# Recommender tower on one Trainium2 core: an early period's layer 0 on VectorE, one unit held back, turnings moved

## The reference, cut to what matters

```python
e = jnp.stack([tbl_0[ids[:, 0]], ..., tbl_31[ids[:, 31]]], axis=1)   # (1024, 32, 16)
x0 = xk = e
for W in (W0, W1, W2):                       # (32, 32, 64), then (32, 64, 64) twice
    xk = relu(einsum('bmd,bhd,mhk->bkd', x0, xk, W))
    outs.append(sum(xk, axis=2))
z = concatenate(outs, axis=1)                # (1024, 192)
h = concatenate([z, dense_ctx], axis=1)      # (1024, 208)
y = relu(relu(h @ W_top1 + b_top1) @ W_top2 + b_top2) @ W_top3
```

## Time and profile before

| | before |
|---|---|
| median of 3 runs | 640.38 us (640.11 to 641.25) |
| profiled execution | 638.23 us |
| its span, first to last instruction | 636.4 us |
| PE busy | 585.1 us, 92% |
| DVE busy | 581.5 us, 91% |
| POOL busy | 443.0 us, 70% |
| ACT busy | 371.1 us, 58% |
| mean granted TensorE clock | 0.984 |

### The profile page before, as it was taken

The page is one execution under the profiler, slowest core; times in us unless marked ns, Lnnn a source line. Parts: engine busy times, 40 slices in busy tenths (PEclk is TensorE's granted clock), DMA queues, the critical chain, the costliest instruction groups (busy, mean ns, idle before and its releaser), DMA issues.

```text
span 636.4 us, 8226 instructions
## 1 busy us (share of the span) xinstructions
PE 585.1 (92%) x3030; PEld 220.0 (35%) x3030; DVE 581.5 (91%) x347; ACT 371.1 (58%) x641; POOL 443.0 (70%) x416
## 2 busy tenths in 40 slices
PE   0678788699898989999999999999999999999998
PEld 0244532233232323333334323333334323334355
DVE  2279976898999999999999999999999999999995
ACT  1147552846756565747676575747676575737551
POOL 6477788797888878886979688886989592703012
PEclk9769999899999999999999999999999999999999
DMA  6663897938293845749291846748391947500000
GB/s 172 183 187 58 318 230 240 340 68 304 60 260 132 214 194 126 283 73 335 49 304 60 212 196 143 266 95 314 61 320 36 233 170 176 234 1 1 0 1 1
DMA packets 33365, 105.85 MB, mean 166 GB/s; under 512 B 8999, under 2 KB 16173, under 8 KB 29485
## 3 DMA queue, kind: packets, MB, share of 16 engines
q1 hardware_dynamic: 24044, 102.72, 51.2%
q0 software_dynamic: 8192, 2.11, 2.7%
q10 hardware_dynamic: 1088, 0.49, 0.4%
HBM read 89.56 MB, written 15.73 MB: 165 GB/s over the span
## 4 chain that ended last, share of the span: by engine, by line
DVE 47%; PE 30%; issue 13%; POOL 7%; DMA 2%; ACT 0%; DVEq 0%; ACTq 0%; POOLq 0%
DVE prod L636 47%; PE accb L757 10%; PE acca L757 9%; POOL emb L470 7%; PE acc L698 3%; DMA emb<-in_table,idx 2%; PE spread L804 2%; PE accb L782 1%; PE acc L782 1%; PE acc L728 1%; PE spread L799 1%; PE spread L800 0%; DMA idx<-in_ids 0%; ACT x1a L959 0%; PE spread L682 0%
## 5 line engine op out<-in xcount | busy, mean ns | idle before, releaser
L470 POOL DMA_INDIRECT emb<-in_table,idx x256 | 244.8, 956 | 81.6 <-issue 68.9
L757 PE MATMUL acca<-prod,w 128*64 128x512 f32 x960 | 215.0, 594 | 4.1 <-DVE prod L636 3.3
L757 PE MATMUL accb<-prod,w 128*64 128x512 f32 x896 | 203.3, 600 | 15.5 <-DVE prod L636 15.5
L636 DVE TENSOR_TENSOR prod<-rows,x1a 128x2048 f32<-128x2048 f32 x64 | 145.5, 2279 | 11.5 <-ACT x1a L959 5.2
L636 DVE TENSOR_TENSOR prod<-rows,x2a 128x2048 f32<-128x2048 f32 x64 | 145.5, 2278 | 5.6 <-ACT x2a L959 4.9
L636 DVE TENSOR_TENSOR prod<-rows,x1b 128x2048 f32<-128x2048 f32 (+1 forms) x65 | 145.5, 2245 | 2.6 <-PE accb L757 1.9
L636 DVE TENSOR_TENSOR prod<-rows,x2b 128x2048 f32<-128x2048 f32 x64 | 145.5, 2278 | 1.1 <-PE accb L757 1.1
L757 PEld LDWEIGHTS acca<-prod,w 128*64 128x64 f32 x960 | 67.2, 137 | 137.0 <-issue 127.0
L757 PEld LDWEIGHTS accb<-prod,w 128*64 128x64 f32 x896 | 61.9, 137 | 149.5 <-issue 107.2
L488 POOL TENSOR_TENSOR prod<-rows,mates 128x1024 f32<-128x1024 f32 x42 | 99.2, 2380 | 4.9 <-DMA rows<-field_dram 4.7
L959 ACT ACTIVATE x1a<-acc 64x512 f32<-64x512 f32 x58 | 33.1, 570 | 95.1 <-PE acc L698 94.4
(11 more groups left out here) (105 smaller groups left out, 349.1 us busy)
## 6 DMA issues: line engine op xcount, KB each, us to landing
rows<-field_dram SPq DMA_DIRECT2D x30, 2048.0 KB, 11.3
field_dram<-zb_field SPq DMA_DIRECT2D x30, 256.0 KB, 3.2
mates<-field_dram SPq DMA_DIRECT2D x15, 512.0 KB, 4.6
across<-field_dram SPq DMA_DIRECT2D x56, 128.0 KB
emb<-in_table,idx POOLq DMA_INDIRECT x256, 4.9
field_dram<-zb_field SPq DMA_DIRECT2D x30, 128.0 KB, 4.1
rows<-field_dram SPq DMA_DIRECT2D x4, 768.0 KB, 7.2
field_dram<-zb_field SPq DMA_DIRECT2D x15, 192.0 KB, 4.4
```

The costliest lines, as they stand in the source:

```text
L470: pool.indirect_dma_start(out=emb[q % EMBS][:, j * EMB:(j + 1) * EMB], out_offset=None, in_=table, in_offset=bass.IndirectOffsetOnAxis(ap= ...
L636: nc.vector.tensor_tensor(prod[:, n % RING, t:t + count, :], of_rows, xs, ALU.mult).then_inc(s_prod, 1)
L757: mm = nc.tensor.matmul(acc[j % 2][side * HID:(side + 1) * HID, :], (w1 if layer == 1 else w2)[:, step, :], prod[:, (made(layer, s, half, ...
```

## The change

- `EARLY_PERIODS` goes from 2 to 3: DVE makes five products for period 2, right after the eight units of slot 2. POOL makes none for it, SP reads neither `across` nor `squares` for it, and ACT squares nothing for it.
- DVE's unit 15, the last of `FIRST_UNITS`, comes after the products of period 1 and not before them, and PE contracts it after the layer 0 of period 1.
- Slot 3's units alternate between the streams, as in the other slots.
- Layer 0 of period 3 is summed one pair earlier on PE: after the first and second pair of slot 4.
- PE turns the fields of period 1 one unit earlier, and those of period 2 inside the layer 0 of period 1, after its second step.
- ACT's `fields_out(1)` comes before `first_input(1, 1, 1)` (the x2b that units 8 and 9 read), and `first_z(2, 1)` after `input1(3, 0)`.
- `keep_busy` on PE: 8 and not 6 after the first turning, one more before the second turning, 3 before unit 0, and 2 after the layer 0 of period 2.

```diff
-    EARLY_PERIODS = 2
+    EARLY_PERIODS = 3
...
-        if j == FIRST_SLOT + 1:
-            return [(*stream, half, u) for half in range(2) for stream in (a, b) for u in range(UNITS)]
...
-    SUM0 = {(FIRST_SLOT, 3): [(k, 2) for k in (*range(L0 - 1), SQUARES, L0 - 1)]}
+    SUM0 = {(FIRST_SLOT, 3): [(k, 2) for k in range(EARLY)]}
...
-        late = q == 3
-        SUM0[2 * q - 2, late] = [(k, q) for k in range(3)]
-        SUM0[2 * q - 2, 1 + late] = [(SQUARES, q), (L0 - 1, q)]
+        SUM0[2 * q - 2, 0] = [(k, q) for k in range(3)]
+        SUM0[2 * q - 2, 1] = [(SQUARES, q), (L0 - 1, q)]
...
-        return q < 2
+        return q < EARLY_PERIODS
...
-            sp.wait_ge(s_prod0p, (PERIODS - 2) * L0)
+            sp.wait_ge(s_prod0p, (PERIODS - EARLY_PERIODS) * L0)
...
             halve12(0)
-            for k in range(L0):
-                product0(2, k)
             gather_early(4)
...
-            for i, unit in enumerate(FIRST_UNITS):
+            for i, unit in enumerate(FIRST_UNITS[:-1]):
                 outer(*unit)
...
             for k in range(EARLY):
                 product0(1, k)
+            outer(*FIRST_UNITS[-1])
             for j in range(FIRST_SLOT, SUBS):
                 for unit in vector_units(j):
                     outer(*unit)
+                if j == FIRST_SLOT:
+                    for k in range(EARLY):
+                        product0(2, k)
...
-            keep_busy(acc[1][:, :], 6)
+            keep_busy(acc[1][:, :], 8)
             pe.wait_ge(s_w0sum, 3)
             for k in range(EARLY):
                 layer0_first(k, 0)
                 if k == 1:
+                    keep_busy(acc[1][:, :], 1)
                     turn_first(1)
-            for i, unit in enumerate(FIRST_UNITS):
+            keep_busy(acc[1][:, :], 3)
+            for i, unit in enumerate(FIRST_UNITS[:-1]):
                 outer_alone(*unit)
...
-                if i == 3 * UNITS - 1:
+                if i == 3 * UNITS - 2:
                     turn_fields(1, 0)
-                if i == len(FIRST_UNITS) - 2:
-                    turn_fields(2, 0)
             for k in order0(1):
                 layer0(k, 1)
+                if k == 1:
+                    turn_fields(2, 0)
+            outer_alone(*FIRST_UNITS[-1])
...
                     for k, q in SUM0.get((j, i), []):
                         layer0(k, q)
+                    if (j, i) == (FIRST_SLOT, 2 * UNITS - 1):
+                        keep_busy(acc[1][:, :], 2)
...
             first_z(1, 0)
+            fields_out(1)
             first_input(1, 1, 1)
-            fields_out(1)
...
             fields_out(2)
-            first_z(2, 1)
             input1(2, 0)
             input1(3, 0)
+            first_z(2, 1)
...
             input2(2, 0)
-            square_fields(2)
             input1(4, 0)
```

More of the change, by code:

```diff
@@ L546, in _ @@
             halve12(LAST - 1)
-            pool.wait_ge(s_prod0p, (PERIODS - 2) * L0)
+            pool.wait_ge(s_prod0p, (PERIODS - EARLY_PERIODS) * L0)
             nc.gpsimd.memset(ones, 1.0).then_inc(s_ones, 1)
```

## The result

The changed kernel takes 632.63 us in the median of 4 runs (632.12 to 633.21), the kernel before 640.25 (639.46 to 641.25). The ratio is 0.988, with a 95% interval of 0.9863 to 0.9897. That is 7.6 us less; 6.0 were forecast, and 632.63 lies 0.6 us under the forecast range. The two profiled executions differ by 6.1 us: 638.23 before, 632.12 after, with spans of 636.4 and 630.3. The forecast for the profiled execution was 632.2, with a span of 630.4. The kernel before has one run more here than in the table ahead of the prediction, which moves its median from 640.38 to 640.25.

A forecast was written before the change was run, and what follows sets the result against it. DVE's row of units was taken to bound the middle, with 15 us of holes before 149.46. Gains of 0.0 + 3.2 + 2.8 = 6.0 us, off the median 640.38, gave 634.4; its own range 633.5 to 635.4, the wider one 633.2 to 638.2.

The forecast's parts named there:

- the last one of the sum: Took the 6.0 us saving off the median of 640.38, which lay 2.15 us above the profiled execution: 634.4.
- part 4: Slots 3 and 4 (110 to 150 us): ring waits go, x1a unit to x1a unit 35.2 for 37.98 us, gain 2.8.
- Part 1: First units (0 to 57 us): clock held, but x2b later; unit 8 begins at 57.2 as before, worth 0.0 us.
- 1.9 us idle are under the 2.4 that cost nothing: PE before slot 3's first pair: an idle stretch of 1.9 us was taken to leave the clock up.
- The rival that hung on the clock: First units: clock does not hold, x2b ready at 58.4, all behind it 1.2 us later, 635.6; chance 0.12.
- Part 2: Held-back unit 15 (57 to 102 us): slot 2's first unit on DVE at 81.2 against 84.46, gain 3.2 us.
- Part 3: DVE's five products after slot 2 (99 to 110 us): cost one unit, 2.2 us, not 5.7; x1a stays at 9.35.
- the reserve of 1 us: Slot 3, E being slot 2's end on DVE: half-clock pair used by E + 17.1, ring first asks at E + 18.1.
- Nothing gave half back: Rival: one new wait, likeliest at part 2's x1a or POOL's product in part 4, gives about 637; chance 0.20.
- DVE's work was not paid in full: Rival: DVE pays all 5.7 us for the products, other holes only move, 0.3 gained, 640; chance 0.05.
- PE did not wait for POOL: Rival in slot 4: PE waits for POOL's third product for period 3; slower, 643 if it comes at E + 42.5; chance 0.03.

The follow-up runs named there:

- e4: The kernel before with no edit, profiled a second time: 640.33 us, span 638.5.
- e5: The kernel before with slot 3 alternating and period 3's layer 0 summed one pair earlier: 634.76 us, against 639.83 for the kernel before.
- e1: The kernel before with the four keep_busy edits and nothing else: 637.57 us, against 639.98 for the kernel before.
- e2: The changed kernel with keep_busy as before the change (6, none, none, none): 632.71 us, ratio 0.9896 to the kernel before.
- e7: The changed kernel with unit 15 back in front of period 1's products on DVE and its layer 0 on PE: 633.83 us.
- e6: The changed kernel with EARLY_PERIODS 2 again, so POOL makes period 2's four products and DVE none: 633.23 us.
- e3: The changed kernel with slot 3 as before, two units of layer 2 and then two of layer 1: 634.55 us.
- The mixed slot 3: The changed kernel with slot 3's first half two units per stream in turn, second half alternating, and keep_busy 5 before the slot: 631.24 us.
- e13: The changed kernel with no further edit, on the second chip with the long TensorE stall: 660.72 us.
- e12: The kernel before with no edit, on the first chip with the long TensorE stall: median 672.91 us, profiled 670.26 us.
- e10: The changed kernel with no further edit, on the first chip with the long TensorE stall: 664.13 us.

## Why the prediction was right and wrong

**The step that failed** is the last one of the sum, "The median is 2.15 us above the profiled execution; I take the saving off it". With it the term of part 4 was mis-sized: 2.8 us, read from one execution of a kernel whose executions range from 637.2 to 643.4 on the chips without the stall. The stretch that part 4 shortens took 37.98 us in that execution and 40.71 in e4, and 35.18 after the change. So the term is 2.8 us for the one and 5.5 for the other, and the spans of e4 and of the changed kernel differ by 8.2 us (638.5 and 630.3). The measured 7.6 lies between 6.1 and 8.2. The prediction kept the distance between median and profile as it was; it fell from 2.0 to 0.5 us, and these 1.5 us are what 7.6 has over 6.1.

How firmly this stands: there are two profiles of the kernel before without the stall, so that its median execution looks like e4 is inferred, from its time and from the granted clocks of 26 executions. e5 has the sign and about the size, 5.1 us in the median. With the 3.4 us of slot 2 that makes 8.5 and not 7.6, so the sizes from different chips fit to about 1 us only. And the clock is not all of the scatter: e1, with every execution at 0.995 or 0.997, still ranges over 4 us.

The sign that could have been read: the profiled execution lay under all three timed ones, and the shown ring waits followed a stretch at half clock. Whoever forecasts a median has to forecast both kernels' scatter, not only the shift of one trace.

**Part 1** came out near zero as forecast: unit 8 at 56.89, against 57.2 reckoned and 57.23 before; DVE's first unit itself started 0.3 us earlier. For the fillers, the rule of the Trainium skill (TensorE: Matmul & The Clock Gate, "Why this matters for your kernels") agrees with the traces in so far as the clock stayed at 1.00 where they shortened the idle stretches, but e1 shows it at 0.50 from 36.7 with the three `keep_busy` in front and 2.78 us idle behind them. The prediction's own "1.9 us idle are under the 2.4 that cost nothing" rests on one row; in e4 the clock fell over the same idle stretch of 2.46 us. The rival that hung on the clock, 1.2 us if it does not hold, was not put to the test: e2 loses nothing in the median, but in its profile the clock was at half only from about 36 to 39.5 among the first four units, and its executions at the lowest clock are 1 to 2 us slower than its median. e1 does not price it either: its 0.8 us at unit 4 are gone at slot 2, but it has the old order, in which DVE waits about 3 us in front of slot 2.

**Part 2** was 3.2 us forecast. From unit 8 to slot 2 it is 3.1 us (27.23 before, 24.13 after); with the 0.3 us of part 1 slot 2 begins 3.4 us earlier (84.46 and 81.02). The hold has 1.8 of it (e7).

**Part 3** was right in place and size: the x1a unit 9.48 us after slot 2's end (108.17 - 98.69) for 9.35, and a hole of 1.24 for 1.3. What it has wrong is whose cost the one unit is. The products do not take it: in e6 they are off DVE, and DVE still fits only one unit before the x1a unit and waits 2.12 us, because the alternating order puts the x1a unit second. In e3, with the products and the old order, both units stand before the x1a unit, which begins 10.2 us after slot 2's end (98.99 to 109.21) and not 9.35: 0.9 us is what the products cost there.

**Part 4** in the trace: no ring wait, 143.35 for 143.5. 35.18 us from the x1a unit of slot 3 to that of slot 5, for 35.2. The ring did not ask too early for PE's first pair even at half clock (e5, e2), but the reserve of 1 us that was reckoned (E + 17.1 for E + 18.1) was not there in e5: the pair was used at about E + 18.1, with E at 102.54. With the clock at full the three ring waits would have been smaller, not gone: e1 has 1.3 us of them, at 121.02 and 130.50.

**The other rivals.** Nothing gave half back; DVE's work was not paid in full; and PE did not wait for POOL, though in e6, with POOL's work added, a wait of 0.54 us for PE came up in slot 5.

**The mixed slot 3** has the lowest median of all versions on the chips without the stall, 631.24. It was not run beside the changed kernel on such a chip, so the 0.8 us between them rests on the profiles and on e7.

## What to carry to other kernels

When the profiled execution lies below the timed ones, ask which of its waits can grow, before taking a saving off the median; a second profile of the same kernel shows one such case. An order in which the consumer's work comes whole at even intervals can do more than keeping the consumer's clock up (here 5.1 us, with the earlier sums, against 2.4): it makes the clock matter less, though not nothing. And work put into a hole is free only if what ends the hole is fixed by another engine; taking it out again, as in e6, is the test.

## What the runs showed of the hardware

GpSimd's gathers (one `DMA_INDIRECT` each) take 0.94 us, but some take about twice that while DVE makes its products of two SBUF tensors (72.28 to 77.95). POOL's timeline after:

```profile
71.27 0.94 POOL L467 DMA_INDIRECT emb<-in_table,idx  x1 [0.30 <-issue]
72.52 1.80 POOL L467 DMA_INDIRECT emb<-in_table,idx  x1 [0.30 <-issue]
74.62 1.97 POOL L467 DMA_INDIRECT emb<-in_table,idx  x1 [0.30 <-issue]
```

The next one, at 76.89, takes 1.97 us too. It is not so for all: beside the five products from 98.61 on, gathers take 1.16, 1.97, 0.94 and 1.09 us. Beside DVE's units, whose x lies in PSUM, none of them takes over 1 us. DVE's products did not slow (1.13 us apart in both kernels). The Trainium skill, GPSIMD Engine Reference, says in its table that GpSimd's SBUF interfaces are shared with VectorE and contend with its instructions that have two SBUF inputs; the trace agrees, at the cost of these gathers.

On three of five chips of the experiments TensorE's instructions came one or two at a time, up to 2 us apart, near 42 to 65 us, in the changed kernel and in the kernel before. PE's timeline and a window of e13:

```profile
54.68 0.59 PE L781 MATMUL acca<-prod,w 128*64 128x256 f32 x1 [0.81 <-issue]
...
59.58 0.58 PE L781 MATMUL acca<-prod,w 128*64 128x256 f32 x1 [1.42 <-issue]
```

```profile
45.30:65.20 19.90, 7.53 (x14) 2.16 (x14) 0.76 (x2) 0.00 (x0) 12.29 (x13) 0.55 0.05 6
```

14 matmul instructions in 19.9 us, with DVE idle, DMA at 0.05 and the operands made long before; DVE then waited 20.70 us for PE's first step in that half. From about 93 to 107 us it happens again, in front of DVE's fifth product of period 1, which waits 12.31 us in e12 and 8.95 and 8.29 in the changed kernel (e10, e13). The two waits together are about the 30 us. The profile names nothing that ended PE's waits. What holds the instructions up, and why on some chips, stays open; it was not tried.
